# Making the mask of the chosen experts on VectorE instead of ACT, in a fused expert-routing and state-space kernel

## The reference

```python
vecs = jnp.einsum('arh,bsh->bsar', A, x)        # 64 experts x 16 numbers per token
arrows = jnp.linalg.norm(vecs, axis=-1)
_, idx = jax.lax.top_k(arrows, TOPK)            # TOPK = 4
routes = jax.nn.one_hot(idx, arrows.shape[-1], dtype=x.dtype).sum(-2) / TOPK
v = jnp.einsum('bsa,bsar->bsr', routes, vecs)
delta = jnp.einsum('bsa,ajr,bsr->bsj', routes, B, v)
base = jnp.einsum('bsh,jh->bsj', x, W) + bias
return base + delta
```

## Time and profile before

| | |
|---|---|
| median of 3 runs | 2952.03 us (2951.98 to 2955.84) |
| profiled execution | 2954.69 us, span 2952.9 us |
| mean granted clock of TensorE | 0.978 |
| scan stage | about 252 us to 2760 us |

### The profile page before, as it was taken

The page is one execution under the profiler, slowest core; times in us unless marked ns, Lnnn a source line. Parts: engine busy times, 40 slices in busy tenths (PEclk is TensorE's granted clock), DMA queues, the critical chain, the costliest instruction groups (busy, mean ns, idle before and its releaser), DMA issues.

```text
span 2952.9 us, 39401 instructions
## 1 busy us (share of the span) xinstructions
PE 2666.8 (90%) x13568; PEld 1201.8 (41%) x13568; DVE 2279.8 (77%) x2915; ACT 1442.5 (49%) x2787; POOL 2346.8 (79%) x703
## 2 busy tenths in 40 slices
PE   4998999999899898889889899999899988888999
PEld 1554444444343343334344344444334433333444
DVE  8434888788878878787888788888787888888533
ACT  5234565555545455554555455455555544454211
POOL 2004999899989998998899899999998999889300
PEclk9999999999999999999999999999999999999999
DMA  5225344544455434444454345444544344344221
GB/s 209 59 60 143 119 132 125 160 136 130 130 141 156 124 105 136 151 130 130 130 157 142 100 127 169 126 132 128 153 137 143 109 148 138 117 133 121 65 58 50
DMA packets 309374, 373.47 MB, mean 126 GB/s; under 512 B 148147, under 2 KB 224051, under 8 KB 309174
## 3 DMA queue, kind: packets, MB, share of 16 engines
q1 hardware_dynamic: 292278, 337.40, 38.5%
q10 hardware_dynamic: 16896, 33.56, 3.8%
HBM read 234.05 MB, written 103.29 MB: 114 GB/s over the span
## 4 chain that ended last, share of the span: by engine, by line
PE 17%; DVE 16%; DMA 8%; POOL 8%; DVEq 8%; ACT 6%; issue 6%; SPq 1%; ACTq 1%; POOLq 0%
DVE mreg L1035 8%; PE pv L488 5%; PE po L488 5%; POOL mreg L456 4%; POOL mreg L448 3%; DVEq L1037 3%; PE pv L492 3%; PE po L492 3%; DMA delta_scratch<-mreg 2%; DMA xin<-x_scratch 2%; ACT pA L832 2%; DMA mreg<-xnT_scratch 2%; DVE pv L1002 2%; DVE sel L1010 1%; PE py L642 1%
## 5 line engine op out<-in xcount | busy, mean ns | idle before, releaser
L456 POOL TENSOR_TENSOR mreg<-mreg 128x2048 f32<-128x2048 f32 x256 | 1161.1, 4536 | 2.6 <-DVE hst L1038 2.6
L832 ACT ACTIVATE pA<-mreg,nA 128x512 f32<-128x512 f32 x1024 | 692.9, 687 | 798.1 <-DVE mreg L1035 720.8
L448 POOL TENSOR_TENSOR mreg<-mreg 128x1024 f32<-128x1024 f32 x340 | 794.8, 2362 | 329.7 <-DMA mreg<-delta_scratch 265.9
L1035 DVE TENSOR_TENSOR_SCAN mreg<-pA,hst,mreg 128x512 f32<-128x512 f32 x768 | 941.2, 1265 | 55.0 <-ACT pA L832 49.0
L488 PE MATMUL po<-wB,uT 128*128 128x512 f16 x2016 | 481.7, 383 | 20.4 <-DMA uT<-sel 20.4
L488 PE MATMUL pv<-wA,xT 128*128 128x512 f16 x2016 | 459.4, 381 | 8.2 <-ACT xT L758 4.2
L488 PE MATMUL po<-wW,xT 128*128 128x512 f16 x2016 | 465.9, 379 | 0.0
L443 POOL TENSOR_TENSOR mreg<-mreg 128x2048 f32<-128x2048 f32 x86 | 390.1, 4536 | 21.5 <-issue 21.3
L1035 DVE TENSOR_TENSOR_SCAN mreg<-pA,cst,mreg 128x512 f32<-128x512 f32 x256 | 313.8, 1265 | 22.9 <-ACT pA L832 21.6
L488 PEld LDWEIGHTS po<-wB,uT 128*128 128x128 f16 x2016 | 189.7, 98 | 326.1 <-issue 129.9
L642 PE MATMUL py<-mreg,Em 128*32 128x512 f32 x2048 | 277.5, 614 | 37.7 <-POOL mreg L456 24.2
(11 more groups left out here) (122 smaller groups left out, 2464.9 us busy)
## 6 DMA issues: line engine op xcount, KB each, us to landing
mreg<-delta_scratch SPq DMA_DIRECT2D x256, 512.0 KB, 5.8
delta_scratch<-mreg ACTq DMA_DIRECT2D x128, 256.0 KB
xin<-x SPq DMA_DIRECT2D x32, 512.0 KB, 4.6
x_scratch<-xin SPq DMA_DIRECT2D x32, 512.0 KB, 3.8
xnT_scratch<-auxs SPq DMA_DIRECT2D x32, 512.0 KB, 2.7
mreg<-xnT_scratch SPq DMA_DIRECT2D x64, 256.0 KB, 7.0
mreg<-bc_scratch SPq DMA_DIRECT2D x64, 256.0 KB, 6.1
yT_scratch<-mreg SPq DMA_DIRECT2D x64, 256.0 KB, 2.3
```

Of the source, the lines that this page charges most:

```text
L448: pool.tensor_tensor(Hr[:, G % NH, 2 * h:2 * h + 2, :], u, b.broadcast_to([P, 2, CT]), ALU.mult).then_inc(s_bm, 1)
L456: pool.tensor_tensor(h, h, Cr[:, g, :].unsqueeze(1).broadcast_to([P, 4, CT]), ALU.mult).then_inc(s_cm, 1)
L832: nc.scalar.activation(pA[:, i % 2, :], Dr[:, 2 * (n % NPR) + i % 2, :], ACT.Exp, scale=nA[:, c:c + 1]).then_inc(s_dA, 1)
L1035: V.tensor_tensor_scan(h, pA[:, i % 2, :], h, before, ALU.mult, ALU.add).then_inc(s_sc, 1)
```

## The change

The mask is formed on VectorE, right behind the replacement, with one tensor_scalar: mask = (n2m < 0). ACT's instruction is gone with its place in ACT's queue, and so are the two semaphores by which VectorE and ACT waited for each other. A drain stands between the replacement and the new instruction, and another at the head of the gather in place of the wait for ACT.

```diff
-            def chosen(a):
-                act.wait_ge(s_n2, a.u + 1)
-                nc.scalar.activation(mask[:, :], n2m[:, 0:NE], ACT.Relu, scale=-1.0).then_inc(s_mk, 1)
-
...
                 if a.u:
                     squares(a, 1)
-                chosen(a)
                 if a.u == 0:
                     weights_b(2, KD)
...
                 V.memset(top[:, TOPK:8], -1.0)
                 dve.drain()
-                dve.wait_ge(s_mk, a.u)
-                V.match_replace(out=n2m[:, :], in_to_replace=top[:, :], in_values=n2[:, :], imm_value=-1.0).then_inc(s_n2, 1)
+                V.match_replace(out=n2m[:, :], in_to_replace=top[:, :], in_values=n2[:, :], imm_value=-1.0)
+                dve.drain()
+                V.tensor_scalar(mask[:, :], n2m[:, 0:NE], 0.0, None, ALU.is_lt)
 
             def gather(a):
                 mask_b = mask[:, :].unsqueeze(2).broadcast_to([P, NE, R16])
-                dve.wait_ge(s_mk, a.u + 1)
+                dve.drain()
                 V.tensor_tensor(sel3, pv[:, :, :].rearrange("p b (a r) -> p (b a) r", r=R16), mask_b,
                                 ALU.mult).then_inc(s_gm, 1)
```

More of the change, by code:

```diff
@@ L216, in build @@
         s_xT = sem("s_xT"); s_xhi = sem("s_xhi"); s_xlo = sem("s_xlo")
-        s_vec = sem("s_vec"); s_sq = sem("s_sq"); s_n2 = sem("s_n2"); s_mk = sem("s_mk"); s_gm = sem("s_gm")
+        s_vec = sem("s_vec"); s_sq = sem("s_sq"); s_gm = sem("s_gm")
         s_u = sem("s_u"); s_uc = [sem(f"s_uc{n}") for n in range(2)]
```

## The result

The changed kernel took 3120.52 us (median of 6 runs, 3098.87 to 3164.14) against 2952.31 us. On another chip the same kernel gave 3156.85 us against 2951.43, ratio 1.067 (1.062 to 1.071). So by the medians it is slower by 168 to 205 us. I had forecast 3022, +70 us, in a range that ended at 3076: the direction was right, the forecast cost was less than half of the measured one, and the time lies outside the range.

A forecast was written before the change was run, and what follows sets the result against it. No single engine was taken as the bound, but a ring of PE, POOL and VectorE with little slack. 37 units at 1.90 us (1.46 stall plus 0.44 added work) gave 70 us, 3022 us at the median; range 2963 to 3076.

The forecast's parts named there:

- What is removed is worth nothing: ACT's 256 ns mask instruction per unit and its wait for VectorE: off the path, since ACT waits behind it anyway.
- Cost without a collision, 0.44 us per unit: VectorE in scan units: 0.26 us for drain and mask before the scans, 0.18 us for the gather's drain.
- The rival without a lock: Mask slips between POOL's accesses, so only the added VectorE work counts: 16 us, 2968 us; chance 0.16.
- The collision with POOL: Scan stage: the two-column SBUF mask instruction and a POOL instruction shut each other out for a whole instruction.
- the length of the stall, 1.46 us per unit: Mask on VectorE waits out the rest of POOL's running instruction; mean over all 53 scan units, estimates 1.24 to 1.76.
- turn-taking: VectorE's L951 and POOL's L432 at the start alternate by whole instructions; L951 goes from 1280 to 3142 ns.
- The share that comes through, 37 of 53 units: 28 of 40 scan-unit starts on the chain, 0.70, so some 37 units carry added VectorE time to the end.
- The range: 2963 to 3076 us; lower end from the case of no lock, upper from all 53 units at 2.20 plus POOL's 10.
- a fixed phase with POOL: Sign of being wrong on the phases: a mean stall under 1 us or over 3 us if the ring settles so.

The follow-up runs named there:

- e3: Changed kernel with no mask: the gather tests or clips n2m itself, no added drain or VectorE instruction, ACT's instruction still gone; 2950.05 us, ratio 0.9989.
- e11: e3 once more with more rounds; 2951.66 us, ratio 0.9994.
- e2: Changed kernel with the same mask, place and drains, but as a scalar_tensor_tensor with its unused second operand in PSUM; 2976.01 us, ratio 1.008.
- e8: e2 with the gather's drain replaced by a wait on a counter of the mask instruction; 2967.70 us, ratio 1.0043.
- e4: Kernel before, mask still on ACT, plus one useless SBUF to SBUF tensor_scalar on VectorE behind the replacement, no drain added; 3131.16 us, ratio 1.059.
- e7: Changed kernel with its mask formed by a tensor_tensor from two SBUF inputs, one column at a time; 3150.98 us, ratio 1.063.
- e1: The changed kernel again, unaltered, for a second profile and its scatter; 3156.85 us.
- e9: Changed kernel with one drain on POOL ahead of every second group, some five products; 3041.88 us, ratio 1.030.
- e5: Changed kernel with a drain on POOL ahead of each of its products; 3087.80 us.
- e10: Kernel before with one drain on POOL ahead of every second group, as in e9; 2959.27 us.
- e6: Kernel before with a drain on POOL ahead of each of its products, as in e5; 3001.43 us.

## Why the prediction was right in direction and wrong in size

- **What is removed is worth nothing:** right. e3 and e11 take ACT's part away and stay within 0.2% of before.
- **Cost without a collision, 0.44 us per unit:** right. The instruction takes 0.195 us where it is free; 0.18 was forecast, though the forecast's own sum, 0.153 + 0.033, is 0.186. The drains' price agrees with e2 and e8 within their intervals. The rival without a lock, 2968 us, was near the price of a kernel that I hadn't been given: e2's is 2976.
- **The collision with POOL:** right as a mechanism. The rate of 0.51 ns per column and the start of the kernel told of it, and e2, e4 and e7 show it.
- **The failed step: the length of the stall, 1.46 us per unit.** It measured 3.86 (204.6/53) and in e1 3.6 (190/53). I read the rows of L951 and L432 as turn-taking and carried it over. But there POOL ran four products in all; in the scan stage it often runs ten and more without a pause (the table above), which I had not counted. In 38 of the 53 units the stall was of the forecast kind, at 1.32 us; the other 15 made three quarters of the sum. The forecast's "each waits until the other's whole instruction is over" holds for short runs alone. In e9, where POOL's runs are kept short, it is 1.39 us per unit, near the 1.46 worked out; in e5 2.1. The 1.46 was read from the phases of the kernel before, and each kernel has its own, so that it came so near in e9 is in part luck. What I should have noted as a rival, with its price, is that the mask never gets its turn until POOL runs dry.
- **The share that comes through, 37 of 53 units:** too low by the times, and in any case the smaller error. The 28 of 40 starts on the chain of before do not tell what else becomes late once VectorE is; in the changed kernel it is 37 of 40. Over the spans: the change 209.5 us of 204.6 + 53 x 0.44 = 228, 92%; e1 200.8 of 214, 94%; e9 against e10 85.5 of 97, 88%; but e5 against e6 99.6 of 135, 74%, where POOL, slowed by its drains, is itself often the late one (31% of e6's chain). With 90% and 1.46 us the forecast would have been 53 x 1.90 x 0.9 = 91 us, near e9's 83, and still about half of the 168 measured.
- **A term left out: the clock.** The shares above put the whole growth down to the stalls and the added work. PE's busy time grew by 44 us in the change, 50 in e1 and 30 in e9 against e10, with the granted clock at 0.949, 0.948 and 0.967. With these taken off the growth, the shares would be 73%, 71% and 57%. Where between the two sets the share lies is open, and so is how much the forecast's 70% was off.
- **The range** took in the phases of one product only, so its upper end (3079 in the sum, 3076 in the range as stated) was the top of the wrong case. The sentence that a fixed phase with POOL could give over 3 us named the number, but not the mechanism (by e1 the pattern is not fixed), and had no chance of its own.

## What to carry to other kernels

Beside a POOL engine that works on SBUF, ask of each VectorE instruction, however small, how many SBUF streams it draws: a second one, by a second SBUF operand or by two columns per step, put it behind POOL's whole instructions here, and a PSUM operand or a fold into a neighbour avoided it. Count how many instructions POOL runs without a pause. Half a POOL instruction was the price only where these runs were short; behind some eight and more, price the time until POOL next pauses, and see whether POOL's pause itself waits for the queue behind the instruction. A share read from the chain of before need not hold for the kernel after: 28 of 40 became 37 of 40 here. And where a stall leaves PE without work, add what its slower clock costs behind it (16 us without work in the example above).

## What the runs showed of the hardware that was not expected

- VectorE's instruction can be passed over at up to five ends of POOL's products in a row, up to 14.3 us (14.7 in e4), for 0.195 us of work. In the change, e1 and e4 every long stall ended where POOL then stood idle; none got in at an end between the first and the last.
- It depends on how long POOL has run: the first end was missed in 2 of 71 cases behind up to 7 products, in 29 of 49 behind 8 to 11, and in 11 of 12 behind 12 or more. One drain on POOL per two groups (0.25 us of idle time) ended that at a price of 6.6 us for the kernel before (ratio 1.0021, 1.0010 to 1.0031).
- A kernel with such a race scatters: 3099 to 3212 us over 10 runs, against 3039.89 to 3043.43 in the four of e9.
- The stall costs a second time through PE: behind the 16.34 us for which PE stood, the granted clock was at its lower level, and eight matmuls took 3.62 us for 1.89.
